# The low part of y for three of four blocks moves from VectorE to GpSimd

## The reference, cut to what matters

```python
proj = x @ w_in.T
q, k, v, a, g = jnp.split(proj, 5, axis=-1)          # heads of 32 columns
q = q * jax.lax.rsqrt(jnp.mean(q * q, axis=-1, keepdims=True) + RMS_EPS)
k = jnp.tanh(k)
a = jnp.clip(jax.nn.sigmoid(a + 2.0), 0.6, 0.9995)
u = k * v
# per chunk of 64 tokens: prefix = cumprod(a), acc = cumsum(u / max(prefix, 1e-6)),
#                         memory = prefix * (state + acc)
gate = jax.nn.sigmoid(g)
y = gate * (q * memory) + (1.0 - gate) * v
return y.reshape(B, S, D) @ w_out.T
```

## Time and profile before

| | |
|---|---|
| runs before | 573.95 to 575.01 us, median 574.57 |
| profiled execution | 573.66 us, span 571.9 us |
| TensorE busy | 507.7 us (89%) |
| VectorE busy | 417.1 us (73%), 778 instructions |
| ScalarE busy | 232.1 us (41%) |
| GpSimd busy | 137.1 us (24%), 145 instructions |
| mean granted clock of TensorE | 0.967 |
| rs on GpSimd, line 1132 | 16 times, mean 3114 ns |
| y_lo on VectorE, line 1444 | 16 times, mean 874 ns |

### The profile page before, as it was taken

How to read it: one execution, slowest core, us unless ns; L and a number is a source line. 1 busy time by engine, 2 the same in 40 slices (tenths; PEclk the granted TensorE clock), 3 DMA queues, 4 the chain that set the end, 5 groups by cost and what they waited for, 6 DMA issues and landing times.

```text
span 571.9 us, 9061 instructions
## 1 busy us (share of the span) xinstructions
PE 507.7 (89%) x3372; PEld 361.8 (63%) x3372; DVE 417.1 (73%) x778; ACT 232.1 (41%) x390; POOL 137.1 (24%) x145
## 2 busy tenths in 40 slices
PE   0557899999899999989999999999998747999997
PEld 0444676567586666758666666866666634677776
DVE  4869887997864777796467788656868568988752
ACT  0145544432814233281422337243342237656540
POOL 5140004254002224401322430133330100321220
PEclk9976999999999999999999999999999877899999
DMA  8994004000002000010200000035535620013112
GB/s 345 409 388 202 1 1 166 1 0 1 37 19 92 2 0 2 1 38 19 92 0 0 0 0 37 18 128 194 188 144 182 216 74 2 19 47 119 41 53 92
DMA packets 15797, 48.21 MB, mean 84 GB/s; under 512 B 1169, under 2 KB 1169, under 8 KB 14225
## 3 DMA queue, kind: packets, MB, share of 16 engines
q1 hardware_dynamic: 15760, 47.73, 22.3%
HBM read 39.34 MB, written 8.39 MB: 83 GB/s over the span
## 4 chain that ended last, share of the span: by engine, by line
PE 65%; DVE 16%; issue 7%; SPq 3%; POOL 3%; DMA 3%; ACT 2%; DVEq 0%; POOLq 0%; ACTq 0%
PE bank L727 9%; PE bank L408 9%; PE bank L732 9%; PE bank L728 9%; PE bank L410 8%; PE bank L409 8%; DMA route_w<-in_switch_w 3%; SPq L434 2%; POOL rs L1132 2%; DVE h_lo L1342 2%; PE bank L531 2%; DVE xt_lo L1353 1%; PE bank L580 1%; PE bank L562 1%; PE bank L638 1%
## 5 line engine op out<-in xcount | busy, mean ns | idle before, releaser
L727 PE MATMUL bank<-xh,win_hi 128*128 128x512 f32 x300 | 133.7, 446 | 0.0
L728 PE MATMUL bank<-xl,win_hi 128*128 128x512 f32 x300 | 118.1, 394 | 0.0
L732 PE MATMUL bank<-xbf,win_lo 128*128 128x512 bf16 x312 | 85.3, 382 | 0.0
L1132 POOL TENSOR_TENSOR rs<-ms,neg_half 128x16 f32<-128x16 f32 x16 | 49.8, 3114 | 137.8 <-ACT ms L950 137.8
L727 PEld LDWEIGHTS bank<-xh,win_hi 128*128 128x128 f32 x300 | 56.4, 188 | 21.0 <-issue 3.2
L728 PEld LDWEIGHTS bank<-xl,win_hi 128*128 128x128 f32 x300 | 56.5, 188 | 11.1
L1119 POOL TENSOR_TENSOR xa<-xa,tables 128x512 f32<-128x512 f32 x28 | 38.9, 1401 | 71.4 <-DVE z_lo L1360 39.0
L408 PE MATMUL bank<-w_hi,z_hi 128*128 128x512 f32 x128 | 51.6, 403 | 0.0
L410 PE MATMUL bank<-w_hi,z_lo 128*128 128x512 f32 x128 | 50.1, 391 | 0.0
L409 PE MATMUL bank<-w_lo,z_hi 128*128 128x512 f32 x128 | 50.1, 391 | 0.0
L732 PEld LDWEIGHTS bank<-xbf,win_lo 128*128 128x128 bf16 x312 | 25.5, 98 | 35.5 <-issue 21.3
(11 more groups left out here) (199 smaller groups left out, 1010.4 us busy)
## 6 DMA issues: line engine op xcount, KB each, us to landing
raw<-in_w_in SPq DMA_DIRECT2D x4, 1280.0 KB, 9.9
route_w<-in_switch_w SPq DMA_DIRECT2D x4, 1280.0 KB, 5.4
route_w<-in_switch_w SPq DMA_DIRECT2D x9, 512.0 KB, 15.5
xa<-in_x SPq DMA_DIRECT2D x4, 1024.0 KB, 5.6
route_w<-in_switch_w SPq DMA_DIRECT2D x2, 2048.0 KB, 15.3
out<-x SPq DMA_DIRECT2D x16, 256.0 KB, 2.0
x_dram<-x1p SPq DMA_DIRECT2D x12, 256.0 KB, 2.0
xa<-x_dram SPq DMA_DIRECT2D x3, 1024.0 KB, 5.7
```

What stands on the lines that cost most here:

```text
L727: pe.matmul(bank[:], win_hi[:, c, r, k, :], xh[:, k, :], start=(k == 0), stop=False)
L728: pe.matmul(bank[:], win_hi[:, c, r, k, :], xl[:, k, :], start=False, stop=False)
L732: mm = pe.matmul(bank[:], win_lo[:, c, r, k, :], xbf[:, k, :], start=False, stop=(k == KC - 1))
L1132: pool.tensor_tensor(rs[:], ms[:], neg_half[:], ALU.pow).then_inc(s_rs, 1)
```

## The change

GpSimd's group gets a fourth part: behind `rs_wide` of block c it makes the low part of block c - 1, for c = 1 to 3. VectorE makes that of block four alone. Since GpSimd now reads `yt`, VectorE waits for it before it overwrites `yt`.

```diff
@@ GpSimd, in group(b, c)
                                    ALU.mult).then_inc(s_rsw, 1)
+                if c >= 1:
+                    y_low(b, c - 1)
+
+            def y_low(b, c):
+                pool.wait_ge(s_yh, KC * b + c + 1)
+                pool.tensor_tensor(y_lo[:, c, :], yt[:], y_hi[:, c, :], ALU.subtract).then_inc(s_yl, 1)
 
             for t in range(NT):
                 route_rstd(t)
@@ VectorE, in group(b, c)
                 ve.wait_ge(s_qn, KC * b + c + 1)
+                if c >= 1:
+                    ve.wait_ge(s_yl, KC * b + c)
                 ve.tensor_tensor(yt[:], qt[:], kt[:], ALU.mult).then_inc(s_qm, 1)
@@ VectorE, in attention
                 for c in range(KC):
                     group(b, c, gap)
                     before(c)
-                    y_low(b, c)
+                    if c == KC - 1:
+                        y_low(b, c)
```

## The result

Median 570.31 us (six runs, 569.25 to 572.36) against 574.43 us for the kernel before (six runs); ratio 0.9933, 95% interval 0.9914 to 0.9952. The prediction was 571.8 us in 569.8 to 573.8, faster. The direction came out, and so did the mechanism in the main; the gain is 4.1 us where 2.8 were forecast.

What follows compares the result with a forecast made beforehand. Bound: TensorE, full inside rows, waits at row ends for what VectorE makes after y. Row ends −2.5, row 0 stall +1.1, last row −1.4 sum to −2.8: 571.8 us against the 574.57 median, range 569.8 to 573.8.

Steps and rivals of the forecast that it cites:

- The bound: Inside a row TensorE is busy throughout; gain comes only where a row ends, when TensorE waits for what follows y.
- The added operation: On GpSimd behind `rs_wide`, 12 subtractions 128x512: 1.30 us each, lower bound 1.04, upper bound 3.11.
- The ends of rows 0 to 2: First hidden product behind block four: TensorE's wait for `xt_lo` goes, −0.93 −0.93 −0.64 = −2.5 us.
- Rival 4: Row ends: the wait goes to ScalarE's table load, then GELU; the 2.5 are lost, 574.3, no change; chance 0.08.
- The stall in row 0: Block three of row 0: the scan runs ahead of `rs_wide`, which ends later, TensorE too: +1.1 us, bounds 0 and 1.4.
- The race in block two of rows 1 and 2: Scan against `rs_wide`, starts 0.1 us apart: taken as 0, upper bound +0.4 twice if the scan is first.
- The last row: Waits for `y_lo` (1.4) and `q_sq` (0.4) go: −1.8; behind TensorE's 4.09 us stop in the routing product, −1.4.
- The sum: Whole kernel: −2.5 + 1.1 − 1.4 = −2.8 us, giving 571.8 us, 0.5% faster; chance 0.50.
- Rival 2: Row 0 costs nothing and the routing product's stop follows y fully: −1.1 −0.5, 570.2 us; chance 0.10.
- The stop ended near 451: Sign in the profile after: TensorE's standstill in the last row's routing product, 4.09 us before, is over near 451.
- rival 5: Ends of rows 0 to 2: the port becomes the bound; at 3.11 us per subtraction +2.3, 576.9, slower; chance 0.07.
- Rival 6: GpSimd holds the port during the pow too; y 0.4 later in three rows: +0.9, 575.5; chance 0.03.

Runs made afterwards that it cites:

- the doubled subtraction: The changed kernel, with GpSimd making the low part of the third block twice, the second behind the first: 572.16 us, ratio 0.9958.

## Why the prediction was right, step by step

- *The bound.* Right in the main: TensorE's projections hide nearly everything inside a row, the gain lies at the rows' ends. The move of eight of twelve subtractions gained 0.44 us (the wait for `q_sq` in row 3, which the prediction had) and cost 0.95 in row 0.
- *The added operation*, 1.30 from the residual add: 1.28, whatever the rounded output. Two of twelve took 2.2 (block two of rows 1 and 2), held up by a scan.
- *The ends of rows 0 to 2*, mis-sized by a term: I counted the one wait in front of the first hidden product (0.93, 0.93, 0.64) and left the others standing. The rows gave 1.15, 1.16 and, in row 0 without its stall, 1.0. What I left out: ScalarE's `y_hi` and the table load behind it move forward with y, so the GELU is no longer late for the second hidden product, and the small second wait for `xt_lo` shrinks from 0.44 to 0.34. In row 1 before, ScalarE and then TensorE:

```profile
243.33 1.28 ACT L854 ACT_TABLE_LOAD   x1
...
246.52 0.50 PE L580 MATMUL bank<-xt_hi,w_hi 64*128 64x512 f32 x2 [0.38 <-ACT hf L874]
```

  After:

```profile
242.18 1.28 ACT L854 ACT_TABLE_LOAD   x1
...
246.53 0.47 PE L408 MATMUL bank<-h_hi,w_hi 128*128 128x512 f32 x1 [0.19 <-DVE h_lo L1348]
```

  TensorE's waits at this row's end were 0.93, 0.38, 0.44 and 0.35 before and are 0.19, 0.34 and 0.36 after, 1.2 us less; the 0.19 for `h_lo` is new, so a small part did pass to another wait. I had named GELU as the next late thing, and had only concluded that it "moves forward too", not that its own wait goes. With the doubled subtraction both waits came back together. Rival 4, which had the waits go over to just that, fell.
- *The stall in row 0*, +1.1: +0.95 (waits of 2.5 against 1.6), by the mechanism that was forecast, the scan ahead of `rs_wide` and the later pow. The forecast's own terms (118.5 + 1.22 + 1.04) end at 120.76 and not at 120.65, so they give +1.2.
- *The race in block two of rows 1 and 2*, taken at 0: GpSimd won it. In row 1:

```profile
201.93 1.04 POOL L1137 TENSOR_TENSOR rs_wide<-rs,ones 128x512 f32<-128x512 f32 x1
202.93 2.20 POOL L1146 TENSOR_TENSOR y_lo<-yt,y_hi 128x512 fp32r<-128x512 f32 x1
...
202.05 2.00 DVE L1427 TENSOR_TENSOR_SCAN pref<-decay,starts 128x512 f32<-128x512 f32 x1
```

  `rs_wide` started 0.12 earlier, kept its 1.04, the scan waited for it (2.00) and then made y_low wait (2.20). TensorE noticed nothing.
- *The last row*, −1.8 at the place and −1.4 behind the stop: −2.2 and −2.24. Two terms of the sum were too small. At the place I took the two waits as the view gives them, 1.4 + 0.4. Counted from the row's first projection y ends 3.0 earlier, where I had 2.5 (434.68 − 371.56 against 439.87 − 373.74), ahead of need, and both waits went. But a listed wait begins at the modelled end of the product before it: here products that start every 0.23 us are shown 0.39 long, so an interruption costs 0.16 more than its wait. The last product before the wait for `y_lo` started at 439.57 and the next at 441.41, 1.84 apart, which is 1.6 lost and not 1.4; the same on the wait for `q_sq` makes 2.1 to 2.2 of the 1.8. And the stop did not hold any of it back: I had allowed it to move only by one hole of 1.0 us in the transfers (440 to 443) and 0.4. The stretch of transfers that ends with the stop starts 60.8 us behind the row's first projection before and 60.5 after, and carries 5.6 MB in both. Before and after (the last two numbers of each line are the DMA engines' busy share and GB/s):

```profile
434.50:452.50 18.00, 12.64 (x186) 10.06 (x185) 14.17 (x28) 5.68 (x8) 3.08 (x8) 0.99 0.90 312
```

```profile
432.10:447.90 15.80, 12.12 (x185) 9.95 (x184) 11.48 (x25) 5.68 (x8) 2.62 (x6) 0.99 0.96 355
```

  The same transfers take 2.2 us less. The gaps are closed, since the last piece of the weights, which waits for y, is issued while the piece before it still runs; but that accounts for about 1.2 us of the 2.2 (10% of 18.0 idle against 4% of 15.8), the rest is a higher rate while busy, which I had not looked at. The bound of −2.0 that I had put was passed by 0.2.
- *The sum.* The terms were too small by 0.2, 0.2 and 0.35 at the ends of rows 1, 2 and 0 and by 0.8 in the last row, and the stall was 0.15 too dear: 1.8 in all. They all err to the same side, and the layer behind the restart and the start gave 0.5 back in the profile. Rival 2, by its figure of 570.2, lies nearest to the measured 570.3, by luck: of its two conditions the stop did follow y, and row 0 did cost its 0.95.
- *Two signs that don't follow from the sum.* "The stop ended near 451" leaves rows 0 to 2 out; with them the sum gives 449.9, and measured were 448.25. And rival 5's sum is slower than before from 2.4 us on, not from 2.55.
- *The page's rule.* Rival 6, the port held by GpSimd for a whole instruction, the pow included, fell: the clip of 229.03 and the scan of 229.70 took 0.43 and 1.23 beside the pow (228.13 to 231.04). For instructions that stream 512 elements the rule of the Trainium skill (page SBUF — State Buffer, section "Who interferes with whom") holds in the rows shown here, but for 0.1 to 0.2 us: the scan of 202.05 ends 1.08 behind `rs_wide` (202.97) and takes 1.22 by itself.

## What to carry to other kernels

Where the matrix engine is full inside a loop, ask of each moved instruction only what it makes earlier behind the last iteration: here one subtraction in three brought nearly all, and the other two brought 0.4 us in the last row and cost 1.0 in the first. An engine that is set free early also takes a shared port early; look for what then starts just behind it on the other engine, and whether that has slack. And when something moves forward, list every wait of the stage that it lies in front of, not the first alone.

## What the runs showed of the hardware

- GpSimd's subtraction of two 128x512 tiles with a rounded output takes 1.28 us, its add without rounding 1.30; VectorE's takes 0.69. A VectorE instruction that meets one of them is lengthened by 0.9 to 1.05 (kt·vt 1.60 and 1.73 for 0.69, a scan 2.27 for 1.22), and the engines then take turns.
- A pow on 128x16 numbers takes 2.91 us on GpSimd and does not stop VectorE's clip or scan beside it; it is itself held up by a VectorE instruction that runs when it starts (4.07 and 4.43 us behind the w_out split).
- TensorE stood still 4.0 us in a long unrolled product with nothing released at the end of it; one load of 1 MB less in front brought 1.5 us instead. In the kernel before it was 4.1 and 1.9. A transfer on the instruction queue is recorded 2.3 to 3.1 us ahead of each restart.
